# A graph network on one core: in the third pass VectorE multiplies a quarter's message before it forms the quarter's one-hots

## The reference, cut to what matters

```
h   = relu(edge_attr @ W1.T + b1)        # 106250 x 96
w   = h @ W2.T + b2
msg = w * x[src]                          # one product per edge and feature
agg = segment_sum(msg, dst)               # summed over the edges of each node
out = relu(x @ Ws.T + bs + agg @ Wn.T + bn)
```

## Time and profile before

| | us |
|---|---|
| median of 3 runs | 4720.6 |
| lowest, highest | 4720.33, 4721.39 |
| the profiled execution's own time | 4718.38 |
| its span, first to last instruction | 4716.6 |
| TensorE busy in the span | 3549.1 |
| VectorE busy | 2500.2 |
| GpSimd busy | 2376.2 |
| mean granted TensorE clock | 0.843 |

### The profile page before, as it was taken

One profiled execution on the slowest core, in us unless ns is written; L12 is line 12 of the kernel. 1 busy time (PEld: TensorE's weight loads), 2 busy tenths in 40 slices (PEclk: granted clock), 3 DMA queues, 4 the chain that ended last, 5 costly groups with the idle time before them and its releaser, 6 DMA issues.

```text
span 4716.6 us, 64730 instructions
## 1 busy us (share of the span) xinstructions
PE 3549.1 (75%) x23472; PEld 2740.7 (58%) x23472; DVE 2500.2 (53%) x6368; ACT 929.8 (20%) x2714; POOL 2376.2 (50%) x2520
## 2 busy tenths in 40 slices
PE   3666776677647777777776676777777789999999
PEld 2444554454424544454444454555555569999999
DVE  4555666565636666666665455555555553232211
ACT  0100000000112222222222232332232230011100
POOL 5566666666466666666664566665565640000000
PEclk6788777777868888888887788878888889999999
DMA  5323232323223333333332222233333338777776
GB/s 148 100 63 73 63 73 65 72 62 73 60 66 104 97 102 98 101 102 106 97 103 67 68 78 70 76 90 93 105 105 103 103 98 267 275 255 257 257 275 241
DMA packets 192519, 555.56 MB, mean 118 GB/s; under 512 B 77782, under 2 KB 83382, under 8 KB 172662
## 3 DMA queue, kind: packets, MB, share of 16 engines
q1 hardware_dynamic: 67132, 335.46, 22.3%
q0 software_dynamic: 80432, 124.45, 12.8%
q10 hardware_dynamic: 44682, 92.08, 5.2%
HBM read 455.53 MB, written 96.37 MB: 117 GB/s over the span
## 4 chain that ended last, share of the span: by engine, by line
PE 46%; another core or an unknown queue 23%; DVE 14%; issue 9%; ACT 5%; ACTq 2%; DMA 1%; DVEq 0%; SPq 0%
PE banks L1443 17%; PE banks L1217 7%; PE banks L1173 5%; DVE scan L2293 5%; PE banks L1245 4%; DVE hot_key L2324 3%; PE banks L1170 3%; PE banks L1357 3%; PE banks L1189 3%; DVE hot_src L2326 2%; PE banks L1365 2%; ACT adj L1710 1%; DVE back L2298 1%; DVE hot_lo L1952 1%
## 5 line engine op out<-in xcount | busy, mean ns | idle before, releaser
L930 POOL DMA_INDIRECT gath<-table,ids x2496 | 2365.8, 948 | 1476.3 <-issue 687.2
L1217 PE MATMUL banks<-back 128*96 128x104 f32 (+11 forms) x6000 | 783.5, 279 | 180.3 <-issue 128.4
L1217 PEld LDWEIGHTS banks<-back 128*96 128x96 f32 x6000 | 721.5, 191 | 253.5 <-issue 185.3
L2324 DVE TENSOR_SCALAR hot_key<-banks,key_t 128x392 bf16<-128x392 int16 x1600 | 658.2, 411 | 315.2 <-remote 292.6
L1443 PE MATMUL banks<-r_parts,adj_in 128*128 128x288 bf16 x6543 | 809.6, 286 | 4.6 <-DMA adj_in<-adjacency 4.6
L1245 PE MATMUL banks<-hot_key,hot_src 128*128 128x392 bf16 x1600 | 459.1, 373 | 468.1 <-ACT adj L1710 292.5
L1443 PEld LDWEIGHTS banks<-r_parts,adj_in 128*128 128x128 bf16 x6543 | 802.4, 143 | 6.4 <-issue 4.4
L2293 DVE TENSOR_TENSOR_SCAN scan<-keep_of,scan,banks 96x512 f32<-96x512 bf16 x414 | 526.3, 1271 | 407.7 <-remote 320.5
L1245 PEld LDWEIGHTS banks<-hot_key,hot_src 128*128 128x128 bf16 x1600 | 149.3, 108 | 786.6 <-issue 726.0
L1173 PE MATMUL banks<-ea_of,w_edge_of 128*96 128x512 f32 x832 | 546.9, 742 | 18.3 <-issue 17.4
L1709 ACT ACTIVATE adj<-banks 128x160 bf16<-128x160 f32 x800 | 242.4, 303 | 1109.8 <-remote 720.3
(11 more groups left out here) (182 smaller groups left out, 2382.5 us busy)
## 6 DMA issues: line engine op xcount, KB each, us to landing
adj_in<-adjacency SPq DMA_DIRECT2D x114, 1568.0 KB, 6.5
adjacency<-adj ACTq DMA_DIRECT2D x100, 464.0 KB
gath<-table,ids POOLq DMA_INDIRECT x2496
ea_of<-in_ea_t SPq DMA_DIRECT2D x78, 512.0 KB
keep_of<-keep_max_d SPq DMA_DIRECT2D x52, 768.0 KB
adjacency<-adj ACTq DMA_DIRECT2D x100, 320.0 KB
adj_in<-adjacency SPq DMA_DIRECT2D x33, 928.0 KB, 4.8
ahead_of<-adjacency SPq DMA_DIRECT2D x33, 640.0 KB
```

The source lines that it names most:

```text
L930: pool.indirect_dma_start(gath[:, b, t, :], None, tables[p][:, :], bass.IndirectOffsetOnAxis(ap=ids[:, 1, n:n + 1], axis=0),).then_inc(s_g ...
L1217: m = pe.matmul(band_ps[g % 2][:, at:at + n], rows_in[:, q % 2, t * D:(t + 1) * D], hot_dst[:, q % 2, t, first:first + n], start=False, st ...
L2324: ve.tensor_scalar(hot_key[:, h, a, :], key_places_ps, key_t[:, 0, a, bass.ds(n, 1)], None, ALU.is_equal)
```

## The change

In `message` the call that forms the one-hots moves from before the waits on `s_w` and `s_gath` to behind the multiplication, and signals `s_hot_end` itself. In `sum_quarter` TensorE waits on that semaphore too; its count goes on from the 416 of the first two passes. Nothing else is changed: the number of VectorE's instructions, their operands and the wait on `s_sel` ahead of both stay.

```diff
                 def sum_quarter(q):
 
                     pe.wait_ge(s_msg, q + 1)
+                    pe.wait_ge(s_hot_end, QUARTERS * 2 + q + 1)
                     to_bands(2, q, msg_now)
...
                     i, k, _ = quarter_of(2, q)
                     if q >= 2:
                         ve.wait_ge(s_sel, sums_marked(2, q - 2))
-                    hots_in_span(q, flag)
                     ve.wait_ge(s_w, q + 1)
                     ve.wait_ge(s_gath[k], 16 * QT * (PAIRS * 2 + i + 1))
                     ve.tensor_tensor(msg_now[:, q % 2, :], wide_w_ps[q % 2],
                                      gath[:, k // 4, QT * (k % 4):QT * (k % 4) + QT, :].rearrange("p t f -> p (t f)"),
                                      ALU.mult).then_inc(s_msg, 1)
+                    hots_in_span(q, flag).then_inc(s_hot_end, 1)
```

## The result

The changed kernel takes 4692.9 us (median of 5 runs, 4687.6 to 4701.3) beside 4720.3 us before (5 runs). The ratio is 0.9945, 95% interval 0.9934 to 0.9956: 0.55% faster, 27 us. The forecast was 4692, in the range 4666 to 4728. The profiled span is 4691.1 us, 25.5 less than before.

What follows compares the result with a forecast made beforehand. The prediction took GpSimd's idle waits for VectorE's message to set the third pass. Terms summed -48 + 20 = -28 us against the profiled 4718.4, giving 4690, with the median 2.2 above: 4692 us, range 4666 to 4728.

Steps and rivals of the forecast that it cites:

- What bounds the pass: Third sparse pass: no engine is full; GpSimd's idle places, 274.6 us in 94 waits for the multiplication, set the pace.
- remote: Profile row of VectorE's waits in the third pass, 422.2 us, read as TensorE's signals arriving late while gathers run.
- The message first: VectorE's message signals 0.51 us earlier in each of GpSimd's 94 waits: 48 us less idle.
- What is given back: GpSimd's earlier restart closes the prompt-signal time sooner, adding 8.5 waits of 2.41 us: 20 us lost, bounds 0 to 48.
- the free stretch: Time after VectorE's release when TensorE's signals still come promptly, 5.5 us; an earlier GpSimd restart closes it sooner.
- The one-hots later: VectorE's two instructions only change places, so TensorE's sum gets both results at the same moment: 0 us.
- TensorE's second wait: 208 more waits on TensorE's queue, priced at 0 of 0 to 14 us because TensorE has 354 us idle.
- rival 3: Faster, but TensorE pays 14 us for its second wait: 4706 us, chance 10%.
- GpSimd's gathers beside other work: Restarted gathers in the third pass now run beside VectorE's one-hots: priced at nothing, bounds 0 to 37 us.
- Nothing moves: Rival: GpSimd's pace and late signals follow from a third thing, so it idles 0.51 us longer later: 4720 us, 18%.
- Slower: Rival: signals that used to slip through are caught, giving GpSimd more idle places: 4744 us, 12%.

Runs made afterwards that it cites:

- e1: Kernel before, one-hots still first but with their own signal, plus TensorE's second wait: 4044.2 us against 4045.4, ratio 1.0000.
- e4: Changed kernel with GpSimd's gathers waiting also for the windows' one-hots behind the message: 4046.6 us, ratio 1.0002 to the kernel before (4045.4).
- e8: Changed kernel with GpSimd's gathers waiting for the one-hots instead of the message, where the kernel before takes 4720.9 us: 4722.8 us, ratio 1.0005.
- e6: Kernel before with one gather a quarter instead of four in the third pass, leaving messages wrong: 4213.1 us, ratio 0.8927 to the kernel before.
- e5: The changed kernel run again, where the kernel before takes 4718.9 us: 4691.1 us, ratio 0.9944.
- e10: Kernel before, one-hots still first but signalling themselves, plus TensorE's second wait, where the kernel before takes 4720.9 us: 4722.8 us, ratio 1.0005.
- e7: Changed kernel with a third one-hot buffer, one-hots formed ahead behind the windows' one-hots: 4693.5 us, ratio 0.9943 to the kernel before.
- e9: Changed kernel with GpSimd's gathers waiting also for the windows' one-hots, where the kernel before takes 4720.9 us: 4857.7 us, ratio 1.0295.
- e11: Changed kernel, message made as one tile then three, GpSimd's first gather waiting only for the first: 4675.6 us, ratio 0.9905 to the kernel before.
- e12: Changed kernel, message made as two tiles and two, each part signalling: 4685.2 us, ratio 0.9930 to the kernel before.
- e2: Changed kernel with GpSimd's gathers waiting for the one-hots instead of the message: 4047.8 us, ratio 1.0005 to the kernel before (4045.4).
- e3: Changed kernel with the quarter's one-hots moved behind the windows' one-hots too: 4046.5 us, ratio 1.0007 to the kernel before (4045.4).

## Why the prediction was right

The number is closer than its parts allow: 4692 for 4692.9, where the changed kernel's own runs lie 14 us apart (4687.6 to 4701.3). That much is luck. It is also bound to the place: it was read from a trace with late signals, and on the chip of e1 to e4, whose traces show none, the kernels with the new order gained nothing. On the chips at 4720 us its steps hold one by one.

**What bounds the pass.** That GpSimd's idle places set its length, though VectorE waits for no gather, was read from two places in the timeline. e8 shows it: only GpSimd's restart was put back, and the 27 us went. e6 shows the other half, that gathers make the signals late; the reading of "remote" was right for this chip.

**The message first, 48 us less idle.** The lag shrank by 0.51 us in the two timelines and by 0.50 in the mean, as worked out. No place is exempt. The number of places was taken as 94.

**What is given back, 20 us.** Measured it is 48 - 27 = 21 us, and GpSimd's idle time is 251.4 us where 247 was worked out (102.5 places of 2.41). The size was right. The row seems to leave the reason in doubt: it has 102 places for the change, but e5, the same kernel in another execution, has

```profile
POOL gath L930 <- DVE back L2477: 243.3, 95, 7.2
```

in 2570 to 3853 us, hardly more than the 94 before. Its places are the idle times whose end the profile gives to VectorE, however short they are. Counted by length over whole traces it comes out: three executions with the old lag (before, e8, e10) have 96, 95 and 96 places of over 1 us, three with the new one (the change, e5, e7) have 105, 103 and 103. From GpSimd's stop to VectorE's release it is 1.6 to 1.7 us in the mean in all six. So there are 8 more places of some 2.5 us, 20 us, as the prediction worked out, and with e9's long lag there are fewer, 80. That the agreement is so close is luck again: counted from 0.4 us it is 108, 110 and 108 places against 117, 111 and 111, 4 more, and GpSimd then waits 0.12 us longer for each release. The direction is shown, more places with a shorter lag, and the total; the share of the two is not. Nor is the reason shown, that the free stretch ends a fixed time after GpSimd's restart, which was read from one place. In e11 and e12 it does not go on in the same way: there are 102 and 101 places of over 1 us, and the wait for the release has grown, to 1.84 and 1.75 us.

**The one-hots later, 0 us; TensorE's second wait, 0 of 0 to 14 us.** Both right: e7 takes the one-hots off everybody's way and gains nothing. e10 has the wait and costs nothing that its interval shows, where rival 3 had 14 us; 7 us is the most that it allows.

**GpSimd's gathers beside other work, 0 of 0 to 37 us.** Right: a median of 947 ns for 944, a maximum of 1230 for 1332.

**The rivals.** *Nothing moves* did not come on the chips at 4720 us. On the chip at 4045 us it was not timed for the change itself, but e2, e3 and e4, which have its order, are all within 0.1% of before. *Slower*: it needed 20 more idle places; there were at most 9 more, by either count.

## What to carry to other kernels

When an engine with plenty of buffers ahead of it still idles, see whether its work disturbs the others; then the way from a late wait's end to its next signal is the path, and what can be formed later should come behind what signals, down to signalling the first part of a result (e11). Price such a move by the wait that it shortens times the number of waits, and take off what comes back as further waits: here 21 of 48 us did. And run it where the disturbance is: on a chip without it, four kernels like these (e1 to e4) differed from the kernel before by less than 0.1%.

## What was not expected of the hardware

The same program took 4045 us on one chip and 4720 us on others. In the third pass TensorE's signals were prompt on the one (no "remote" row for VectorE or ScalarE) and microseconds late on the others, as long as GpSimd issued four gathers a quarter, 5.0 us of issuing in about 6.3 us. With one gather a quarter they were prompt there too (e6), in the same execution in which the first two passes still had them late. Why one chip has it and the other does not, and which part of a gather does it (writing its descriptors, its packets, its completions), no run here tells.
